# A transformer layer with f32 attention output: each head's output kept with its columns in partitions

## What is computed

```python
xn = layernorm(x)                                   # no weights
q, k, v = split(xn @ w_qkv.T); q, k = rope(q), rope(k)
attn = softmax((q @ k.T) / 4)                       # per head, 2048 x 2048
y = x + (attn @ v) @ w_out.T + (silu(xn @ wg.T) * (xn @ wu.T)) @ wd.T
```

## Time and profile before

| | us |
|---|---|
| median of 3 runs (3313.52 to 3319.1) | 3315.56 |
| the profiled execution | 3318.81 |
| its span in the profile | 3317.0 |
| PE busy | 3069.1 (93%) |
| DVE busy | 2855.9 (86%) |
| ACT busy | 2461.4 (74%) |
| POOL busy | 332.0 (10%) |
| DMA, mean of 16 engines on SP's queue | 11.6% |

### The profile page before, as it was taken

The page is one execution under the profiler, slowest core; times in us unless marked ns, Lnnn a source line. Parts: engine busy times, 40 slices in busy tenths (PEclk is TensorE's granted clock), DMA queues, the critical chain, the costliest instruction groups (busy, mean ns, idle before and its releaser), DMA issues.

```text
span 3317.0 us, 67219 instructions
## 1 busy us (share of the span) xinstructions
PE 3069.1 (93%) x20120; PEld 953.3 (29%) x20120; DVE 2855.9 (86%) x3362; ACT 2461.4 (74%) x4701; POOL 332.0 (10%) x544
## 2 busy tenths in 40 slices
PE   5888885799999999999999999999999999999999
PEld 3555553122222222222222222222222222222227
DVE  6676673999999999999999989898989898989953
ACT  4444443488888888888888888887888888888882
POOL 2544544000000000000000000000000000000000
PEclk9999998699999999999999999999999999999999
DMA  2222222100000000000000000000000000000006
GB/s 92 77 92 82 76 95 65 25 24 23 20 23 19 24 19 23 20 22 21 21 21 21 21 21 21 21 21 21 21 21 21 21 21 21 21 21 21 21 2 190
DMA packets 86697, 118.82 MB, mean 36 GB/s; under 512 B 13568, under 2 KB 73600, under 8 KB 86400
## 3 DMA queue, kind: packets, MB, share of 16 engines
q1 hardware_dynamic: 86400, 114.91, 11.6%
HBM read 79.76 MB, written 33.55 MB: 34 GB/s over the span
## 4 chain that ended last, share of the span: by engine, by line
issue 79%; DVE 6%; PE 5%; POOL 4%; ACT 2%; DMA 0%; POOLq 0%; DVEq 0%; SPq 0%; ACTq 0%
PE psum L607 2%; POOL qk_rot L851 1%; DVE row_max L1227 1%; PE psum L526 1%; ACT silu L747 1%; POOL parts L857 1%; PE psum L549 1%; DVE xn L977 1%; POOL hT L863 1%; DVE y_blk L1117 1%; PE psum L667 1%; DVE h L1108 0%; DVE rot_s L1095 0%; DVE stats L930 0%; POOL stab L912 0%
## 5 line engine op out<-in xcount | busy, mean ns | idle before, releaser
L1227 DVE TENSOR_REDUCE row_max<-psum 128x1 f32<-128x1024 f32 x2048 | 2401.0, 1220 | 176.5 <-PE psum L624 159.5
L808 ACT ACTIVATE probs<-psum 128x512 f32<-128x512 f32 x4096 | 2135.4, 604 | 412.7 <-PE psum L683 335.5
L683 PE MATMUL psum<-q_op,k_op 51*128 51x512 f16 x4096 | 1265.8, 388 | 44.4 <-ACT probs L808 18.2
L624 PE MATMUL psum<-k_op,q_op 48*128 48x512 f16 x4096 | 1048.4, 393 | 91.2 <-issue 36.8
L667 PE MATMUL psum<-probs,v_op 128*32 128x512 f32 x8192 | 1114.9, 617 | 9.2 <-ACT probs L808 0.7
L683 PEld LDWEIGHTS psum<-q_op,k_op 51*128 51x128 f16 x4096 | 315.5, 94 | 1383.9 <-ACT probs L808 1232.5
L624 PEld LDWEIGHTS psum<-k_op,q_op 48*128 48x128 f16 x4096 | 215.9, 94 | 383.7 <-DVE row_max L1227 290.2
L907 POOL TENSOR_TENSOR neg_unit<-neg_max,unit 128x16 f32<-128x16 f32 x64 | 14.5, 227 | 2541.9 <-DVE neg_max L1201 2541.9
L667 PEld LDWEIGHTS psum<-probs,v_op 128*32 128x32 f32 x8192 | 163.7, 108 | 261.2 <-issue 246.3
L740 ACT ACTIVATE parts<-qk_rot 128x512 f16<-128x512 f32 x64 | 40.3, 629 | 244.5 <-POOL qk_rot L851 244.5
L526 PE MATMUL psum<-xnT,w 128*128 128x512 f16 x768 | 184.3, 387 | 10.1 <-DVE h L1108 10.1
(11 more groups left out here) (108 smaller groups left out, 1138.7 us busy)
## 6 DMA issues: line engine op xcount, KB each, us to landing
qk_dram<-staged SPq DMA_DIRECT2D x64, 256.0 KB, 2.9
q_op<-qk_dram SPq DMA_DIRECT2D x128, 128.0 KB
k_op<-qk_dram SPq DMA_DIRECT2D x128, 128.0 KB
x_ln<-in_x SPq DMA_DIRECT2D x16, 512.0 KB, 3.5
x_res<-in_x SPq DMA_DIRECT2D x16, 512.0 KB, 4.2
y_dram<-y_blk SPq DMA_DIRECT2D x16, 512.0 KB, 3.0
k_op<-qk_dram SPq DMA_DIRECT2D x128, 64.0 KB
q_op<-qk_dram SPq DMA_DIRECT2D x128, 64.0 KB
```

What stands on the lines that cost most here:

```text
L624: mm = pe.matmul(bank(2 * half + j), q_op[r:r + ROWS, s, t * P:(t + 1) * P], k_op[r:r + ROWS, s, cols:cols + BANK], start=True, stop=True)
L683: pe.matmul(bank(b), k_op[r:e, h % SLOTS, t * P:(t + 1) * P], q_op[r:e, h % SLOTS, j * BANK:(j + 1) * BANK], start=True, stop=True).then_i ...
L808: nc.scalar.activation(probs[:, g2 % 2, j * BANK:(j + 1) * BANK], bank(b), ACT.Exp, scale=to_score).then_inc(s2_used, 1)
L1227: nc.vector.tensor_reduce(row_max[:, hl % 2, t, half:half + 1], psum[:, 2 * half * BANK:(2 * half + 2) * BANK], AX.X, ALU.max).then_inc(s1 ...
```

## The change

The output of a head keeps its columns in partitions. TURN, NORM, the gather and all transposes of stage C are gone. `acc_sb` has two buffers. After SAVE of head h, `place_output(h)` on SP sends the four rows of 512 sums to `sums`, [128, 16] (four DMAs); DVE takes their reciprocal at `INV_AT`, three steps after SAVE; SP stores it to DRAM, waits, and loads it from there spread over 16 partitions a quarter (four DMAs); GpSimd multiplies (`divide`); SP copies the four quarters to their rows of `oT_of(n)`, where PE can use them as the stationary operand (four DMAs). GpSimd also copies v into `v_op` in DVE's place. SP calls `place_output(h - 1)` after `load_stab(h)` and `load_head(h + 2)`; its program and GpSimd's are written out, not loops. The transposed maxima count as two items of the ring of three (`STAB_ITEMS`), so that a head still has 66. `PRO` becomes 39, and `STEPS_B` 1048. `y_in` has eight buffers, filled before the last head, and DVE adds into it in place. From step 1025 on PE projects a tile of 128 tokens per step (`project`), and DVE adds two tiles every second step; the last sequence's four blocks wait for the last head.

```diff
+        def place_output(h):
+            n, m = divmod(h, H)
+            u = h % 2
+            sp.wait_ge(acc_saved, h + 1)
+            for j in range(4):
+                sp.dma_start(sums[32 * j:32 * j + 32, :], acc_sb[32 * j + DH:32 * j + DH + 1, u, :]).then_inc(sums_moved, 16)
+            sp.wait_ge(sum_inv, h + 1)
+            sp.dma_start(inv_dram[0, :].rearrange("(p c) -> p c", c=TILES), inv_sum[:, :]).then_inc(inv_stored, 16)
+            sp.wait_ge(inv_stored, 16 * (h + 1))
+            for j in range(4):
+                sp.dma_start(inv_rows[32 * j:32 * j + DH, :],
+                             inv_dram[:, j * BANK:(j + 1) * BANK].to_broadcast([DH, BANK])).then_inc(inv_spread, 16)
+            sp.wait_ge(o_ready, h + 1)
+            row = m * DH % P
+            for j in range(4):
+                sp.dma_start(oT_of(n)[row:row + DH, m * DH // P, j * BANK:(j + 1) * BANK],
+                             acc_sb[32 * j:32 * j + DH, u, :]).then_inc(o_placed, 16)
...
+        sp.wait_ge(b_const, 7)
+        for h in range(HEADS):
+            load_stab(h, 0)
+            if h + 2 < HEADS:
+                load_head(h + 2, 0)
+            if h >= 1:
+                place_output(h - 1)
+            if h == HEADS - 2:
+                for k in range(Y_BUFS):
+                    load_y(k)
+        STORED_EARLY = 4
+        for k in range(STORED_EARLY):
+            store_out(k)
+            if k >= 1:
+                load_y(k - 1 + Y_BUFS)
+        place_output(HEADS - 1)
+        for k in range(STORED_EARLY, NBLK):
+            store_out(k)
...
+        def project(q):
+
+            k, t = divmod(q, BLK)
...
+            if t == 0:
+                pe.wait_ge(o_placed, 64 * H * (k // BLK + 1))
...
+                mm = pe.matmul(psum[:, 2 * (k % 2) * BANK + t * D:2 * (k % 2) * BANK + (t + 1) * D],
+                               oT_of(k // BLK)[:, c, tok * P:(tok + 1) * P], woT[:, c, :], start=(c == 0), stop=(c == KT - 1))
...
--            h = head_of(c, TURN_AT)
-            if h is not None:
-                pe.wait_ge(acc_saved, h + 1 + SLOTS * i)
-                b = take_bank(item)
-                for n in range(4):
-                    mm = pe.transpose(bank(b)[:, n * P:(n + 1) * P], acc_sb[:, n * P:(n + 1) * P], ident[:, :])
-                mm.then_inc(s2_full, 1)
-                item += 1
...
+            if c > N1:
+                project(c - N1 - 1)
...
             if h is not None:
                 act.wait_ge(pv_done, TILES * (h + 1 + SLOTS * i))
-                nc.scalar.activation(acc_sb[:, :], bank(7), ACT.Copy).then_inc(acc_saved, 1)
+                if h >= 2:
+                    act.wait_ge(o_placed, 64 * (h - 1 + SLOTS * i))
+                nc.scalar.activation(acc_sb[:, h % 2, :], bank(7), ACT.Copy).then_inc(acc_saved, 1)
...
+            h = head_of(c, INV_AT)
             if h is not None:
+                dve.wait_ge(sums_moved, 64 * (h + 1 + SLOTS * i))
+                if h >= 1:
+                    dve.wait_ge(inv_stored, 16 * (h + SLOTS * i))
+                nc.vector.reciprocal(inv_sum[:, :], sums[:, :]).then_inc(sum_inv, 1)
...
+        for h in range(HEADS):
+            copy_v(h)
+            split_max(h, h == 0)
+            if h >= 1:
+                divide(h - 1)
+        divide(HEADS - 1)
```

More of the change, by code:

```diff
@@ L192, in layer_program, with oT_of @@
     stabT = sb(sB, "stabT", [STAB_PARTS * TILES, P], F16)
[L193 to L200, removed]
+    acc_sb = sb(sB, "acc_sb", [P, 2, BANK])
+    sums = sb(sB, "sums", [P, TILES])
+    inv_sum = sb(sB, "inv_sum", [P, TILES])
+    inv_rows = sb(sB, "inv_rows", [P, BANK])
+    oT_first = sb(sB, "oT_first", [P, KT, TILES * P])
+    y_in = sb(sB, "y_in", [P, Y_BUFS, BLK, D])
     sB.close()
+    def oT_of(n):
+        if n == 0:
+            return oT_first[:, :, :]
+        return v_space[:, (n - 1) * TILES * D:n * TILES * D].rearrange("p (k n) -> p k n", k=KT)
     psum = keep.enter_context(nc.psum_tensor("psum", [P, 8 * BANK], F32))
@@ L285, in layer_program @@
     SAVE_AT = FIRST2 + TILES + 1
[L286 to L291, removed]
+    INV_AT = SAVE_AT + 3
+    STEPS_B = N1 + (INV_AT - TILES) + 1
+    STAB_ITEMS = 2
+    HEAD_ITEMS = 4 * TILES + STAB_ITEMS
     assert HEAD_ITEMS % RING == 0
-    PRO = NORM_AT
+    PRO = INV_AT
     BODIES = (N1 - PRO) // UNROLL
@@ L421, in _ @@
         load_head(1, 0)
[L422 to L448, removed]
+        sp.wait_ge(b_const, 7)
[16 more added lines that the diff above has]
+            store_out(k)
+            if k - 1 + Y_BUFS < NBLK:
+                load_y(k - 1 + Y_BUFS)
+        for b in range(Y_BUFS):
+            sp.wait_ge(res_out[b], 16 * (NBLK // Y_BUFS))
     @block.tensor
@@ L585, in _ @@
         pe.wait_ge(partsT_saved, BLK * NBLK)
[L588 to L591, removed]
+        def project(q):
+            k, t = divmod(q, BLK)
+            if q == 0:
                 pe.wait_ge(s1_used, 2 * N1)
-            if not first:
-                pe.wait_ge(cT_saved, KT * (k - 1))
-            for c in range(KT):
[L596 to L610, removed]
+            if t == 0:
+                pe.wait_ge(o_placed, 64 * H * (k // BLK + 1))
+            if k >= 2 and t % 2 == 0:
+                pe.wait_ge(res_ready, 2 * (k - 2) + t // 2 + 1)
+            tok = k % BLK * BLK + t
+            for c in range(KT):
+                mm = pe.matmul(psum[:, 2 * (k % 2) * BANK + t * D:2 * (k % 2) * BANK + (t + 1) * D],
+                               oT_of(k // BLK)[:, c, tok * P:(tok + 1) * P], woT[:, c, :], start=(c == 0), stop=(c == KT - 1))
+            if t % 2 == 1:
+                mm.then_inc(proj_full, 1)
         def max_half(c, i, half):
@@ L685, in step @@
                     item += 1
-            if c == FIRST_C:
-                for j in range(2):
-                    turn_o(0, j, True)
+            if c > N1:
+                project(c - N1 - 1)
         run_steps(pe, step)
[L693 to L703, removed]
+        for q in range(STEPS_B - N1 - 1, NBLK * BLK):
+            project(q)
     @block.scalar
@@ L791, in step @@
                     act.wait_ge(stab_loaded, 32 * (h + SLOTS * i))
[L792 to L801, removed]
+                b = arrived(item, STAB_ITEMS)
+                nc.scalar.activation(stabT[:, :], bank(b).bitcast(F16)[0:STAB_PARTS * TILES, 0:P], ACT.Copy).then_inc(s2_used, STAB_ITEMS)
+                item += STAB_ITEMS
             g2 = c - FIRST2
@@ L812, in _ @@
         run_steps(act, step)
[L815 to L827, removed]
     @block.gpsimd
@@ L1167, in _, with add_y @@
         dve.wait_ge(b_const, 7)
[L1169 to L1183, removed]
-                                        y_in[:, j, 2 * u:2 * u + 2, :], ALU.add).then_inc(res_ready, 1)
-        def save_first():
-            for j in range(2):
-                for c in range(KT):
-                    dve.wait_ge(cT_full, KT * j + c + 1)
-                    nc.vector.tensor_scalar(oT[:, j, c, :], bank(2 * j + c), 1.0, None, ALU.mult).then_inc(cT_saved, 1)
+        def add_y(half):
+            k, u = divmod(half, 2)
+            b = k % Y_BUFS
+            if u == 0:
+                dve.wait_ge(yin_loaded[b], 16 * (k // Y_BUFS + 1))
+            dve.wait_ge(proj_full, half + 1)
+            nc.vector.tensor_tensor(y_in[:, b, 2 * u:2 * u + 2, :], bank(2 * (k % 2) + u).rearrange("p (t d) -> p t d", t=2),
+                                    y_in[:, b, 2 * u:2 * u + 2, :], ALU.add).then_inc(res_ready, 1)
         def step(c, i):
@@ L1228, in step @@
                                             AX.X, ALU.max).then_inc(s1_used, 1)
-            if c == FIRST_C:
-                dve.wait_ge(o_ready, H)
-                for j in range(2):
-                    gather(0, j, True)
-                save_first()
-        run_steps(dve, step)
-        dve.wait_ge(o_ready, HEADS)
-        for j in range(2):
-            gather(1, j, False)
-            add_y(0, j, True)
-        with dve.Fori(1, NBLK // 2 - 1) as n:
-            for j in range(2):
-                gather(n + 1, j, False)
-                add_y(n, j, False)
-        for j in range(2):
-            add_y(NBLK // 2 - 1, j, False)
+            if c > N1 and (c - N1) % 2 == 0:
+                add_y((c - N1) // 2 - 1)
+        run_steps(dve, step)
+        for half in range((STEPS_B - N1 - 1) // 2, 2 * NBLK):
+            add_y(half)
     keep.close()
```

80 lines of the change are left out of this document (38 added, 42 removed).

## The result

The changed kernel takes 3370.0 us (median of 4 runs, 3364.9 to 3372.0) against 3317.3 us: 1.54% slower, ratio 1.0154 with a 95% interval of 1.0141 to 1.0167. The forecast was 3435 us. It is slower as forecast, and inside the range, but by 53 us where 119 were forecast.

The account below looks back on a forecast made before the run. The prediction took the ring between PE and ACT to bound a plain step, DVE only 0.01 us behind. It summed 3318.8 - 36.5 + 108 + 66 - 21 = 3435 us, range 3335 to 3530.

Parts of the forecast that it names:

- ring: Loop between PE and ACT that sets a plain step; removing work from it nets -0.57 us a head, -36.5 for 64.
- DVE's wait: Before the reciprocal, DVE waits for the sums' DMAs behind load_head's loads: net +2.3 us a head, +108 for 47.
- half clock: PE stops while DVE waits, and its granted clock falls to 0.50: +1.4 us a head, +66 for 47.
- end: After the last head's SAVE: tiles projected beside the last head shorten what follows, -21 us.
- Part 1: Plain steps and TURN: TURN goes, -0.81 us a head; transposed maxima lengthen a step by 0.24; net -0.57.
- Part 2: Sums' DMAs queue on SP behind loads on two engines; DVE waits before the reciprocal, +2.3 us, 47 heads, +108.
- Part 3: PE's clock falls after its stop during DVE's wait: +1.4 us a head, +66 for 47 heads (0 to 216).
- rival (b): DVE's wait for the sums is there, but PE's clock holds: 3369 us; chance 0.25.
- in those the wait is covered: At 14 loop-backs PE is already empty at that step, so DVE's wait adds nothing; 47 of 61 heads pay.
- Part 4: Kernel's end: a tile projected per step after the last maximum, last head's chain covered; -21 us (bounds -27 and -13).

Follow-up runs that it names:

- spread loads: Changed kernel with each of the four loads of a head that have an outer dimension of two cut in two, twelve loads for eight: 3226.4 us, ratio 0.9728.
- a later reciprocal: Changed kernel with the reciprocal two steps later, INV_AT = SAVE_AT + 5, loads left on two engines: 3228.9 us, ratio 0.9742.
- GpSimd's queue: Changed kernel with the four sums' DMAs issued by GpSimd ahead of its division, no longer by SP: 3233.8 us, ratio 0.9750.
- the change with both: Changed kernel with loads cut to twelve of 64 KB and all 1048 steps written out, no loop: 3160.5 us, ratio 0.9526 to the kernel before.

## Why the prediction was wrong in size

In spans: forecast 3317.0 + 116.5, measured 3317.0 + 52.1. Term by term:

| term | forecast | measured | from |
|---|---|---|---|
| ring, 64 heads | -36.5 (-0.57 each) | -42 (-0.65 each) | 38.89 a head with spread loads |
| DVE's wait, 47 heads | +108 (+2.3) | +92 (+1.96) | 18 heads at full clock, 40.85 |
| half clock, 47 heads | +66 (+1.4) | +54 (+1.14) | mean of all 47, 41.99 |
| loop-back heads, 14 | 0 beside the ring | -29 (-2.04) | 45.75 to 43.06, less the ring |
| end | -21 | -23 | 123.4 to 100.3 |
| start of the stage | 0 | -1.5 | 615.7 to 614.2 |
| sum | +116.5 | +50.5 | the spans: +52.1 |

**Part 1** held. TURN and SAVE came out at the value worked out (5.80 to 5.00 for 0.80 of 0.81); the ring's shortening cost 0.16 and not 0.24. DVE's relief brought nothing by itself, as said: 0.80 less 0.16 is the whole 0.64 to 0.65 that a head lost.

**Part 2** held in its mechanism, its place and its heads. DVE came 14.4 us after load_stab (forecast 14.5), the sums 16.1 after (forecast 16.8): the loads ended some 15 us after it in this head, not 16.3, and the small DMAs added about 1 us and not 0.5. The wait is 2.1 us in a plain head, and costs it 1.96. 16 us of the miss.

**Part 3** held in the main: in 29 of 47 heads, not in each, the clock fell to 0.50, with stops of PE of 1.0 to 1.9 us; in the other 18 it stayed at 1.00 with stops of 0.8 to 1.8. The table's 1.14 us come nearly all from the clock and not from longer waits: DVE waited 2.06 us at the mean in the 18 heads, 2.08 in the 17 with a short stretch at half clock (42.10 us long), 2.28 in the 12 with one twice as long (43.54). That the shorter stop leaves the clock alone, rival (b), is refuted, though its number, 3369, is the measured one: the right time by a wrong reason. 12 us of the miss.

**The step that failed** is the sentence of part 2 on loop-backs, "in those the wait is covered", with what it leaves out. Covered it was: these heads took 43.06 us with the wait, and 43.66, 42.84 and 43.41 where spread loads, a later reciprocal or GpSimd's queue had removed it or nearly so. But the sum then has no term for these 14 heads beside the ring's: it keeps the price of a loop-back, 6.2 us over a plain head, as it was, without a reason. Measured, the loop-back heads went from 6.2 over a plain head of before to 3.5, because the price depends on the loads under way. In the kernel before, the loop-back stands in the midst of the loads' time on two engines (12 us after load_stab), and ACT restarts after 5.3 us; one step later, 14 us after it, it stands at the end of that time, and ACT restarts after 3.4. The kernel before with the body one step later shows the same by itself, 45.75 to 43.98. Over these fourteen heads the granted clock is 0.96 where it was 0.92. That is 29 us of the miss, half of the 61 us too much in the heads. The prediction had a row that could have raised the question: the earlier trace rows, 10.2 us at half clock after PE's stop of 2.40, and ACT's stop of 5.28 us beside it, the row shown above, which it only called "longer". That the price would fall, no row of before said.

**Part 4** held: 2.9 us a step where 2.84 was worked out, PE's tiles behind it at 0.86 (forecast 0.905), the end 4.1 us after the last addition; the last head's chain was covered: its last DMA was sent 12.6 us after SAVE, and PE never waited for it. One figure of its bounds is off: 17 transfers of 512 KB are 8.9 MB and 37 us at 242 GB/s, not 8.5 and 35; the sum does not use it.

## What to carry to other kernels

A small DMA that an engine on the critical path waits for was here as late as the loads before it in its queue, for the sake of two sixteenths of its data. Before moving data by small DMAs, look at how long the queue's loads run at a share that is a small number of engines of sixteen, and cut those loads so that they spread, or use another queue, or ask later; each of the three took the wait away here, or all but 5 us of it. A wait of 2 us in an engine that was only just hidden cost 3.1 us a head, because PE's clock followed PE's stop. And what a loop's turn costs is worth a look in the trace: here writing the steps out was worth as much as the change, and the change with both (3160.5 us) is 4.7% faster than the kernel before.

## What the runs showed of the hardware that was not expected

- Stops of PE of no more than 1.0 to 1.9 us went with a fall of the granted clock to 0.50 in 29 of 47 heads; a head then took 1.3 us more, or 2.7 where the clock stayed low for longer. Heads with the same stop can go either way: 18 stayed at 1.00 with stops of 0.8 to 1.8 us.
- A loop-back with 64 steps in the body costs 4 to 5 us of a head when no load is under way (42.8 to 43.7 against 38.9 to 39.6), and 6.2 to 6.3 when loads occupy two DMA engines (45.75 against 39.53, 45.21 against 38.88).
- The same 768 KB take 15 us in eight loads, four of which run on two engines, and under 10 us in twelve that spread, for the same time on SP.
- Of a small DMA behind such loads in the same queue, fourteen sixteenths of the packets ran at once and two sixteenths behind the loads, 3.5 us later; from another queue these two sixteenths ran among the loads' packets, 0.5 to 3 us behind the rest.
